# Moving the output projection and the first residual's statistics one slot later in a post-norm transformer layer

## The reference

```python
qkv = x @ Wqkv + bqkv
q, k, v = jnp.split(qkv, [D, D + KV], axis=-1)          # D = 256, KV = 64
scores = jnp.einsum('bqhd,bkhd->bhqk', q, k) / HD       # HD = 16, k and v tiled to 16 heads
prob = jax.nn.softmax(scores, axis=-1)
att = jnp.einsum('bhqk,bkhd->bqhd', prob, v).reshape(b, s, D) @ Wout + bout
x = layernorm(x + att)
gate, up = jnp.split(einsum('bsd,hd->bsh', x, ternary(w_gate_up)), 2, axis=-1)   # 1024 each
h = silu(gate) * up
y = einsum('bsh,dh->bsd', rms_norm(h), ternary(w_proj))
x = layernorm(x + y)
```

## Time and profile before

| | |
|---|---|
| median of 3 runs | 559.68 us (559.02 to 562.63) |
| the profiled execution's own time | 559.17 us |
| its span, first to last instruction | 557.2 us |
| PE busy | 521.8 us, 94% of the span |
| DVE busy | 443.0 us, 80% |
| ACT busy | 363.6 us, 65% |
| POOL busy | 332.5 us, 60% |
| granted PE clock, mean | 0.982 |

### The profile page before, as it was taken

The page is one execution under the profiler, slowest core; times in us unless marked ns, Lnnn a source line. Parts: engine busy times, 40 slices in busy tenths (PEclk is TensorE's granted clock), DMA queues, the critical chain, the costliest instruction groups (busy, mean ns, idle before and its releaser), DMA issues. The chain is left out here.

```text
span 557.2 us, 13565 instructions
## 1 busy us (share of the span) xinstructions
PE 521.8 (94%) x4152; PEld 444.7 (80%) x4152; DVE 443.0 (80%) x1009; ACT 363.6 (65%) x735; POOL 332.5 (60%) x511
## 2 busy tenths in 40 slices
PE   4687999999999999999999999999999999999884
PEld 4677778788888888888888888888888888776773
DVE  6877796868888887878797878888898888875784
ACT  4553774657576767676777767676777676767553
POOL 4566774245665756575756656656657565656744
PEclk9896999999999999999999999999999999999997
DMA  9777173616253636354454536162627162010001
GB/s 233 133 153 121 45 138 74 115 58 115 51 107 57 131 55 135 69 124 79 106 98 95 105 83 117 65 119 57 121 41 164 16 152 51 22 41 1 19 21 38
DMA packets 83395, 49.16 MB, mean 88 GB/s; under 512 B 39696, under 2 KB 83344, under 8 KB 83344
## 3 DMA queue, kind: packets, MB, share of 16 engines
q1 hardware_dynamic: 81456, 47.87, 41.7%
q10 hardware_dynamic: 1888, 0.66, 0.5%
HBM read 33.29 MB, written 14.68 MB: 86 GB/s over the span
## 5 line engine op out<-in xcount | busy, mean ns | idle before, releaser
L867 DVE TENSOR_REDUCE row_max<-short_ps 128x2 f32<-128x512 f32 x256 | 169.8, 681 | 37.1 <-PE short_ps L579 35.7
L1055 POOL TENSOR_TENSOR h_lo<-h_f,h_hi 128x256 fp32r<-128x256 f32 x116 | 85.5, 737 | 163.9 <-ACT h_hi L766 163.7
L794 ACT ACTIVATE probs<-exp_ps 128x1024 f32<-128x1024 f32 x128 | 130.8, 1022 | 41.7 <-PE exp_ps L588 41.3
L579 PE MATMUL short_ps<-k_st,q_st 65*128 65x256 f32 x512 | 108.5, 296 | 3.8 <-DVE row_max L867 3.4
L775 ACT ACTIVATE tanh<-ffn_ps 128x256 f32<-128x256 f32 x120 | 45.9, 383 | 89.3 <-PE ffn_ps L607 89.3
L579 PEld LDWEIGHTS short_ps<-k_st,q_st 65*128 65x128 f32 x512 | 88.3, 193 | 15.2 <-issue 2.5
L1060 POOL TENSOR_TENSOR sq_sum<-sq_sum,h_sq 128x256 f32<-128x256 f32 x111 | 83.1, 749 | 7.0 <-ACT h_sq L830 6.7
L588 PE MATMUL exp_ps<-q_st,k_st 67*128 67x512 f32 x256 | 81.5, 400 | 3.4 <-DMA q_st<-shift_lo 3.2
L607 PE MATMUL ffn_ps<-x1T_hi,wguT 128*128 128x256 f32 x480 | 80.0, 289 | 3.7 <-DVE h_f L953 3.5
L620 PE MATMUL down_ps<-wpT,h_hi 128*128 128x256 f32 x256 | 79.4, 332 | 3.9 <-DVE h_lo L856 2.9
L607 PE MATMUL ffn_ps<-x1T_lo,wguT 128*128 128x256 f32 x480 | 77.9, 285 | 0.0
(11 more groups left out here) (110 smaller groups left out, 834.5 us busy)
## 6 DMA issues: line engine op xcount, KB each, us to landing
q_st<-q_dram SPq DMA_DIRECT2D x128, 128.0 KB, 3.9
q_dram<-q_p SPq DMA_DIRECT2D x16, 512.0 KB, 3.0
k_st<-k_dram SPq DMA_DIRECT2D x64, 64.0 KB, 2.4
res<-in_L_attn_x_dram SPq DMA_DIRECT2D x16, 256.0 KB, 2.8
xn<-in_L_attn_x_dram SPq DMA_DIRECT2D x62, 64.0 KB, 2.8
out_dram<-y_out SPq DMA_DIRECT2D x15, 256.0 KB, 2.9
wgu_raw<-in_L_ffn_w_gate_up_dram SPq DMA_DIRECT2D x8, 256.0 KB, 6.1
k_dram<-k_p SPq DMA_DIRECT2D x16, 128.0 KB, 2.5
```

The costliest lines, as they stand in the source:

```text
L579: last = pe.matmul(bank[:, t * S:(t + 1) * S], q_st[0:PAD, st.par, head, t * P:(t + 1) * P], k_st[0:PAD, st.par, st.s % 4, :], start=True, ...
L794: act.activation(probs[:, st.s % 4], exp_ps[:], ACT.Exp).then_inc(exp_done, 1)
L867: dve.tensor_reduce(row_max[:, st.par, head * TT:(head + 1) * TT], short(n, f"max{i}")[:].rearrange("p (t k) -> p t k", t=TT), AX.X, ALU.m ...
L1055: pool.tensor_tensor(h_p[1][:, st.s % 4, :], h_f[:, st.s % 2, :], h_p[0][:, st.s % 4, :].bitcast(F32), ALU.subtract).then_inc(h_lo, 1)
```

## The change

`PROJ_O` moves from offset 26 to 27, and in PE's code from behind the products with values (where it stood, in slot 2, there are none) to ahead of them; `O_ADD` moves with it to 27, `RSTD1` from 27 to 28, and in POOL's code from behind `h_lo` and `sq_sum` to ahead of them. `LN1_APPLY` and all later steps stay where they are. The banks of slot 4 are exchanged, so that `r1_done` is waited for by `max_scores` 1 and not by `max_scores` 0. No instruction is added or removed; ACT and SP keep their order.

```diff
-PROJ_O = 26
+PROJ_O = 27
 LN1_APPLY = 28
...
-O_ADD = 26
-RSTD1 = 27
+O_ADD = 27
+RSTD1 = 28
...
-SHORT_ORDER = ("max0", "q", "max1", "sq", "k", "shift0", "o", "shift1", "v", "x1")
+SHORT_ORDER = ("max0", "q", "max1", "o", "sq", "k", "shift0", "shift1", "v", "x1")
...
-              2: {"max0": 0, "max1": 2, "q": 1, "o": 0},
-              3: {"max0": 2, "max1": 1},
-              4: {"max0": 0, "max1": 2, "k": 1},
+              2: {"max0": 0, "max1": 2, "q": 1},
+              3: {"max0": 2, "max1": 1, "o": 0},
+              4: {"max0": 2, "max1": 0, "k": 1},
```

More of the change, by code:

```diff
@@ L682, in slot @@
                     max_scores(n, st, 1)
+                if st := n.once(PROJ_O):
+                    bank = use_short(n, "o")
+                    wait(pe, att_turned, st.count(2, 2))
+                    if st.it is None and st.b == 0:
+                        pe.wait_ge(wo_loaded, 16 * (2 * G + 1))
+                    for t in range(TT):
+                        last = products(bank[:, t * D:(t + 1) * D], [attT[:, m, t * P:(t + 1) * P] for m in range(DT)],
+                                        [wo[:, m, :] for m in range(DT)])
+                    last.then_inc(o_made, 1)
                 if (st := n.chunk(PV0)) and st.s % 2:
@@ L709, in slot @@
                     turn_maxima(bank, st, 0)
[L710 to L718, removed]
                 if st := n.once(SHIFT_T[1]):
@@ L1050, in slot @@
                         normalised(pool)
+                if st := n.once(RSTD1):
+                    wait(pool, var1_done, st.count(TT, TT))
+                    pool.tensor_tensor(ve1[:], mv1[:, :, 1], ln_eps[:], ALU.add).then_inc(ve1_done, 1)
+                    wait(pool, ve1_done, st.count(1, 1))
+                    rsqrt(rstd1[:], ve1[:], rstd1_done)
+                    wait(pool, rstd1_done, st.count(1, 1))
+                    pool.tensor_tensor(mean1[:], mv1[:, :, 0], minus_one[:], ALU.mult).then_inc(mean1_done, 1)
+                    wait(pool, mean1_done, st.count(1, 1))
+                    pool.tensor_tensor(shift1[:], mean1[:], rstd1[:], ALU.mult).then_inc(shift1_done, 1)
                 if st := n.chunk(H_LOW0):
@@ L1061, in slot @@
                                            ).then_inc(h_summed, 1)
[L1062 to L1070, removed]
                 if st := n.once(INV):
```

## The result

The changed kernel takes 576.04 us, the median of four runs from 574.98 to 577.67; the kernel before, run beside it, 559.7 us. The ratio is 1.028, with an interval from 1.024 to 1.033. The forecast was 573.0, with a range from 567 to 577. The profiled execution took 577.67 us (a span of 575.7), 18.5 more than that of before.

What follows compares the result with a forecast made beforehand. PE's queue was taken as the bound. Waits in the middle (8.7 us) and the last elements (4.9 us) summed to 13.6 us on 559.17, giving 572.8, stated as 573.0 us; range 567 to 577.

Steps and rivals of the forecast that it cites:

- The bound, and where to look: PE's queue is the bound, busy 94% of the span; look at slot 2, where DVE works unbroken up to `h_f`.
- The wait in the middle, 11 x 0.79 = 8.7: Slot 3's `gate_up` waits for slot 2's `h_f`, 0.79 us in each of eleven middle elements, 8.7 us in all.
- The price of the projection by starts: On PE in slot 2, the output projection costs 1.73 us by instruction starts, against 1.89 us by busy time.
- Statistics, roots and banks at nothing: Slots 3 and 4: moved DVE statistics covered by 0.88 us, POOL work by 2.1 us, bank exchange covered; no cost.
- The unseen pair at zero: Float32 projection straight ahead of the products with values, absent from the trace: taken as zero, 1.5 us either way.
- The last elements, 1.7 + 1.7 + 1.5 = 4.9: Projection no longer hidden in waits: slots 131 and 139 each 1.7 us longer, last norm 1.5 us later; 4.9 us.
- The end absorbs its part: Rival: the middle's wait comes, but slack in the last norm's chain absorbs the end's part; 568.4 us, chance 0.07.
- the middle doesn't pay: Rival: only the last elements cost, since `h_f` is early enough in the middle; 564.6 us, chance 0.05.
- Not slower: Rival: PE's work is only permuted, 559.7 us, chance 0.05; or small waits go too, 554.5 us, chance 0.03.
- the estimate of 0.4 us for slots 6 and 7: PE's small waits in slots 6 and 7, 0.4 us an element in 13 elements, might go: 5 us gained.
- More than forecast: Rival: DVE's statistics or the projection's result come late, delaying slot 4; 0.4 us in 11 elements, 577.5 us, chance 0.10.
- the forecast's own bounds: Whole kernel at 570 to 575.5 us, from the wait's bounds and 1.5 us of the unseen pair; chance 0.70.

Runs made afterwards that it cites:

- Experiment 4: Changed kernel with DVE's `LN2_STATS` moved behind slot 2's second row maximum for all elements but the last; 560.67 us, ratio 0.9995.
- experiment 1: Changed kernel with projection, add and statistics at their old places in the last three elements; 568.91 us, ratio 1.011.
- Experiment 9: Changed kernel with the projection's first token tile kept in slot 2 and only its second in slot 3; 562.53 us, ratio 1.003.
- experiment 5: Changed kernel with the projection back in slot 2 on PE; add, statistics, roots and banks stay as changed; 560.93 us, ratio 1.001.
- experiment 2: Changed kernel with the new order only in the last three elements, new bank table in every slot; 567.05 us, ratio 1.009.
- Experiment 3: Changed kernel with an extra, unread q projection of eight entries on PE in slots 130 and 138; 572.67 us, ratio 1.019.
- experiment 6: Kernel before with POOL's second norm roots (`RSTD2`) moved from offset 44 to 45, a slot later; 561.72 us, ratio 1.002.
- the other alone: Kernel before with only DVE's `LN2_STATS` moved behind slot 2's second row maximum; 565.14 us, ratio 1.008.

## Why the prediction came out as it did

- **The bound, and where to look.** Right. PE's queue sets the pace, and the wait for `h_f` in slot 3 is where the time went: 3.5 us became 13.0. Experiment 4 removes it without touching the projection, and the time is back.
- **The wait in the middle, 11 x 0.79 = 8.7.** Right in place, count and size. 0.76 inside the loop and 0.82 outside, for 0.74 and 0.83 forecast; 8.8 by the slots, 8.4 by the medians of experiment 1. Inside the loop the first four entries behind a wait took 0.10 us more than usual, not the 0.07 that the working carried over from outside it; the row at 338.75 already reads 0.74 for 0.64. The two numbers that gave it held: `h_f` begins 4.28 us after the slot's first `gate_up`, and the slot without the projection takes 4.10 (experiment 4). Experiment 9 confirms it from the other side: half of the projection moved stays under the 1.12 us that DVE left, and costs nothing there.
- **The price of the projection by starts, 1.73 and not the busy time's 1.89.** Right: slot 3 grows by 1.73 in experiment 4. The busy time would have made the wait 0.16 longer.
- **Statistics, roots and banks at nothing.** Right in the middle: experiments 5 and 2 show no step there.
- **The unseen pair at zero.** Right. From the projection's start to the products' are 1.82 us (361.87 to 363.69): the 1.73, and 0.09 extra at the entry into the products.
- **The last elements, 1.7 + 1.7 + 1.5 = 4.9.** The mechanism is right and the term too small: 3.15 + 4.7 + 1.5 = 9.4 in the profiled execution, less by the runs of experiment 2 (6.6 by the medians). "The projection was hidden in slot 2 and is not in slot 3" counted what it costs where it arrives, and nothing for where it left. There it had also kept PE at work within the wait. Without it the wait is 2.3 us, PE's clock falls to half, and the work behind the wait is slower by 1.5 and 3.0 us. Experiment 3 shows this directly: filled with work that nobody reads, the slots grow by just 1.62 and 1.72. The term had nothing for the clock, though the trace of before holds such a case that wasn't read: at 38.9 us PE waits 2.31 us for DVE's `row_max`, and the granted clock is 0.50 from 41.8 to 45.2 us. The last norm was right as a sum, though experiment 5 gives about 1.0 of its 1.5 to the later add and roots.
- **The rivals.** "The end absorbs its part" and "the middle doesn't pay" both fell, since experiments 1 and 2 find a price for each alone. "Not slower" fell, and with it the estimate of 0.4 us for slots 6 and 7: experiment 6 shows a round of 2.59 us there, which stays when POOL's work is moved away. "More than forecast" had the right sign and the wrong place: it expected DVE's statistics to be late in slot 4, and they are not. The measured 576.04 lies just above the forecast's own bounds, 570 to 575.5. That the wider range held it is luck: a rival with another mechanism had widened it, and the clock wasn't foreseen.

The sum was 13.6 us; with the end as measured it is 18.1 (8.7 + 9.4). The medians differ by 16.3, and the profiled executions by 18.5 with 0.8 of chance in slot 31 and 0.5 lost in slot 89 of before. What fixes the time from start to slot 31, which varied by 2.6 us between the profiled executions (100.2 to 102.8 us), and whether the DMA that lands late in some of them is the same thing, stays open.

## What to carry to other kernels

Work that stands in a wait can be worth more than its own length (here, in the last elements, 3.15 and 4.7 us for 1.7 each): before you move it, ask what the engine does in that place afterwards, and whether PE's clock survives it. To find what a move on one engine uncovers, measure from the first instruction of the slot to the release it waits for (here 4.71 us to the end of `h_f`) and compare it with the slot's length once the work is gone (4.10); half of the work may fit where the whole doesn't. Two moves on two engines can belong together: here one alone costs 2.8%, the other alone 0.8%, and both nothing.

## What the runs showed of the hardware

- Waits of 2.31 and 2.34 us in an otherwise busy kernel were enough for PE's granted clock to fall to 0.5, with PE busy for 2.1 of the 4.4 us before. In the kernel before, the waits at those places were 0.24 and 0.75 us and it stayed at 1.00; it did so too with 1.13 us left beside the filler, with 1.62 us in experiment 9, and with 1.74 us at 539.9 us of the kernel before. The length of the wait alone doesn't tell: at 39.2 us of the changed kernel the clock fell behind a wait of 1.71 us.
- The fall came between 0.3 us before PE was at work again and 1.6 us after. The time at half clock was 3.4 us at slot 131 in three executions (the changed kernel twice, experiment 2), and 6.8, 3.4 and 6.8 us at slot 139.
- Wholly within half clock an instruction took not quite twice as long: the last four entries of `gate_up` 0.86 us for 0.48 (513.65 to 514.51), `exp_scores` 0.85 for 0.47, the projection 3.55 for 1.82.
- A start of PE behind a wait for `h_f` came 0.06 us after its end inside the hardware loop and 0.15 outside it, and the first four entries took 0.10 and 0.07 us more; the eleven middle elements repeated these values within 0.01 us. Why the two differ isn't shown.
- One 8 KB DMA (`q_st<-shift_lo`) landed in 1.9 us in five of the thirteen profiled executions and in 2.9 to 3.7 us in the other eight, among them three kernels with the old order at that place, and lengthened its slot by 0.7 to 1.5 us.
